# Row order of a gated FFN's hidden values, sums for the norms gathered by other instructions, and x quantised between a weight's steps

## The chip, the cores and the metric

The kernel runs on one core of a Trainium2 chip. The metric is the device time of one launch in microseconds (us). The core has a matmul engine (TensorE, PE in the profile), a vector engine (VectorE, DVE), a scalar engine (ScalarE, ACT), GpSimd (POOL) and SyncE (SP), which here only issues transfers. Each engine works through its own list of instructions in order; they wait for each other on semaphores.

## The reference, cut to what matters

Thirty-two sequences of 512 tokens with 256 channels go through two fake-quantised feed-forward blocks with a state-space layer between them.

```python
def fp4_quant_dequant(x):           # blocks of 16 along the last dimension
    xb = x.reshape(shape[:-1] + (shape[-1] // 16, 16))
    scale = max(max(abs(xb)) / 6.0, 1e-12)
    q = GRID[searchsorted(MID, abs(xb / scale))] * sign(xb) * scale
def fp4_linear(x, w): return fp4_quant_dequant(x) @ fp4_quant_dequant(w).T
def ffn(x): return fp4_linear(silu(fp4_linear(x, w_gate)) * fp4_linear(x, w_up), w_down)   # 256 -> 704 -> 256
def ssm(x):                          # 16 states a channel, a scan over 512 tokens
    Bm, Cm = split(x @ W_in + b_in); dt = softplus((x @ W_dt1 + b_dt1) @ W_dt2 + b_dt2)
    h[t] = exp(A * dt) * h[t-1] + expm1(A * dt) / A * Bm * x;  return sum(h * Cm) + D * x
x = x + 0.5 * ffn(layernorm(x)); x = x + ssm(layernorm(x)); x = x + 0.5 * ffn(layernorm(x))
```

A layernorm here subtracts the mean of a token's 256 channels and divides by sqrt(variance + 1e-5).

## The kernel before, in words

**Start.** SP loads the constants, the three weights and the first x. DVE quantises `w_gate`, `w_up` and `w_down` one after the other (L645 to L722), PE transposes each, ACT and DVE split the result into a high and a low f16 part. GpSimd finds the largest scale over all partitions by `partition_all_reduce` (L464, L468, L470, L475) and takes one power (L472). Only then does `body(-1, ...)` run on each engine: the first x is normalised and quantised, SP transposes it (`turn_x`), and PE begins its first product (L1200).

**Iterations.** After that there are 34 iterations. An iteration holds five stages of different sequences: A, the first FFN of sequence `it`; R, the norm and the small projections of the same sequence; S, the scan of sequence `it - 1`; C, the second FFN of sequence `it - 2`; N, load, norm and quantisation of the x of sequence `it + 1`. The first iterations lack S and C, the last ones lack A, R and N. The order of the work is written out by hand in `ORDER`, one list of pieces an engine: `A.am2`, say, is piece 2 of `am` (the maxima of the hidden values) in stage A. Every engine walks its list once an iteration.

**A norm.** DVE takes `bn_stats` of four groups of 128 tokens (L768), aggregates them (L774), and makes variance plus epsilon (L776) and the negated mean (L777), all in `stats`. GpSimd raises the variance to -1/2 and multiplies (`norm`, L481, L483). ACT writes the normalised x (`normalise`, L1017). There are three norms for a sequence: f (N and C, buffers `f_...`) and s (R, buffers `s_...`).

**Quantisation of the hidden values.** DVE multiplies gate and up into `hid` (`hidden`, L823), which lies by position: element `i` of all 44 blocks, then element `i + 1` of all. This comes from the order in which the rows of `w_gate` and `w_up` are loaded (L378). `amax_h` (L828) takes a maximum over each block, `scales_h` scale and reciprocal, GpSimd multiplies by the reciprocals (`values_h`, L529) and rounds by adding and taking off a magic number (`round_h`, L537, L545), and the grid value times the scale's high part (DVE, `high_h`, L846) and low part (GpSimd, `low_h`, L560) gives `qh`. SP transposes `qh` (`turn_h`) for the product with `w_down` (L1214). DVE adds the residual (`ffn_residual`, L857).

**The rest of R and S.** PE transposes the norm's output into `gu_ps` (L1224), projects (L1230), and ACT takes the result (`take_rBC`, L1057). DVE splits C into a high part (L882) and a low part (L885) in `split_C`, and `times_B` multiplies C and B (L875). Softplus and `make_dt` give dt. For each of 16 states and 2 halves, PE makes differences (L1274), ACT a decay (L1104), DVE the scan (L912) and the product with C (L922), PE adds it up in `y_ps` (L1294). At the end `take_y` adds `x_s` (L931). The bank pair `gu_ps` is shared by all gate and up products, the transposes of R and its projections; a new A begins when `dt` is made.

Of the kernel before, what the change touches and what calls it, by code (L numbers as in the profile page):

```python
# [28 lines left out]
    S.k0 S.c0 S.k1 A.gu0 S.w0 S.w1 A.gu1 S.w2 A.gu2 S.e0 S.w3 A.gu3 S.w4 S.w5 S.c1 S.e1 S.p0 S.w6 A.gu4 A.gu5  # L29
    S.p1 A.gu6 S.c2 S.p2 S.p3 S.w7 S.w8 S.p4 S.p5 S.c3 A.gu7 S.w9 C.gu0 S.w10 S.c4 S.p6 S.p7 C.gu1 S.p8 A.dn0  # L30
    S.w11 S.w12 A.dn1 S.c5 C.gu2 C.gu3 S.w13 S.c6 S.p9 C.gu4 A.dn2 S.w14 S.w15 A.dn3 C.gu5 S.p10 S.c7 S.p11
    S.p12 S.p13 S.p14 S.w16 S.w17 S.c8 C.gu6 S.w18 C.gu7 S.w19 S.c9 R.xt0 S.w20 S.p15 S.p16 S.p17 S.w21 S.w22
# [4 lines left out]
    S.k0 S.k1 C.ln0 A.hid0 S.g0 S.g1 A.hid1 C.xa0 C.xa1 C.xs0 S.p0 A.hid2 S.g2 S.g3 S.p1 C.xm0 S.g4 C.xm1 A.am0
    A.hid3 A.am1 S.p2 A.qs0 A.hid4 S.g5 S.p3 A.hid5 S.g6 C.qy0 C.qy1 A.qm0 S.p4 S.p5 A.qm1 S.g7 A.hid6 S.g8
    A.qv0 A.hid7 A.am2 S.p6 S.p7 C.hid0 A.am3 A.qs1 A.qv1 S.p8 S.g9 S.g10 A.qm2 S.p9 A.res0 A.qm3 S.g11 C.hid1
    S.g12 A.qv2 C.am0 A.res1 C.hid2 S.p10 S.p11 C.hid3 C.am1 A.qv3 C.qs0 S.g13 C.hid4 S.p12 S.p13 A.res2 S.g14  # L40
# [1317 lines left out]
```

## Time and profile before

| | |
|---|---|
| median of 3 runs | 3940.95 us (3935.68 to 3943.92) |
| the profiled execution | 3939.07 us, its span 3937.3 us |
| DVE busy | 3663.4 us, 93% |
| PE busy | 3345.5 us, 85% |
| GpSimd busy | 2834.5 us, 72% |
| ACT busy | 2735.2 us, 69% |
| mean granted TensorE clock | 0.956 of full speed |

Busy time is the union of an engine's instructions. A matmul's end is modelled, so that PE's busy time is not time at its peak. The whole span holds a start of some 120 us, in which little overlaps, then the iterations.

### The profile page before, as it was taken

What the parts mean: (1) busy time and instruction counts of PE and PEld (TensorE: products, weight loads), DVE (VectorE), ACT (ScalarE), POOL (GpSimd) and SP (SyncE); (2) the same over time, 40 slices, a digit from 0 to 9 for tenths busy, and PEclk for the clock granted to TensorE, in tenths of its full rate; (3) what the DMA queues carried; (4) which work ended last, traced back from release to release, by engine and by line L of the source; (5) the groups of instructions that cost most, each with busy time, mean ns of one, the idle gap of its engine ahead of it and who ended that gap; (6) DMA issues with size and microseconds to landing.
All of it is one profiled execution on the core that took longest, in us unless ns stands there. A gap on an engine that the chain in (4) does not pass through costs nothing. (4 is left out here: it accounts for less than half of the span.)

```text
span 3937.3 us, 79115 instructions
## 1 busy us (share of the span) xinstructions
PE 3345.5 (85%) x28716; PEld 2377.4 (60%) x28716; DVE 3663.4 (93%) x6091; ACT 2735.2 (69%) x5258; POOL 2834.5 (72%) x2296
## 2 busy tenths in 40 slices
PE   0478988988998888889889888988889988888985
PEld 0256666666666666666666666666666666666663
DVE  6489999999999999999999999999999999999995
ACT  0267777777677777777777777777777777777772
POOL 1447777787777778777777877777877777787755
PEclk9789999999999999999999999999999999999997
DMA  1111222222222222222222122222222222322212
GB/s 30 28 32 43 56 47 49 57 44 52 52 55 52 47 60 41 55 52 55 49 49 60 40 56 52 47 52 55 44 52 56 51 52 47 60 42 54 47 37 45
DMA packets 583041, 192.04 MB, mean 49 GB/s; under 512 B 544061, under 2 KB 578302, under 8 KB 582654
## 3 DMA queue, kind: packets, MB, share of 16 engines
q1 hardware_dynamic: 582654, 186.98, 23.3%
q8 instruction: 230, 3.77, 0.4%
q14 instruction: 157, 1.29, 0.1%
HBM read 19.16 MB, written 16.78 MB: 9 GB/s over the span
## 5 line engine op out<-in xcount | busy, mean ns | idle before, releaser
L1200 PE MATMUL gu_ps<-wgu,qxT 128*128 128x352 f16 x6144 | 1093.0, 329 | 197.5 <-DVE hid L823 94.8
L912 DVE TENSOR_TENSOR_SCAN state<-w_ps,decay 128x512 f32<-128x512 f32 x1024 | 1212.3, 1207 | 35.1 <-ACT decay L1104 22.8
L1200 PEld LDWEIGHTS gu_ps<-wgu,qxT 128*128 128x128 f16 x6144 | 587.2, 102 | 621.9 <-DVE hid L823 162.2
L1274 PE MATMUL w_ps<-bdif,x_parts 128*128 128x129 f16 (+1 forms) x12288 | 858.6, 224 | 78.6 <-DVE state L912 70.6
L1274 PEld LDWEIGHTS w_ps<-bdif,x_parts 128*128 128x128 f16 x12288 | 775.0, 100 | 170.7 <-issue 134.5
L1104 ACT ACTIVATE decay<-dt,A_sb 128x512 f32<-128x512 f32 x1024 | 677.8, 712 | 128.7 <-DVE state L912 101.1
L922 DVE SCALAR_TENSOR_TENSOR c_state<-state,inv_A,rep_ps 128x512 f32<-128x512 f32 x1024 | 726.2, 735 | 1.6 <-PE rep_ps L1284 0.4
L498 POOL TENSOR_TENSOR bdif<-dif,B_lo 128x516 f16<-128x516 f16 x512 | 531.6, 1055 | 188.9 <-PE w_ps L1274 188.9
L1092 ACT ACTIVATE bdif<-dif,B_tok 128x129 f16<-128x129 f16 x2048 | 629.1, 394 | 0.9 <-PE w_ps L1274 0.9
L1294 PE MATMUL y_ps<-ident,c_state 128*128 128x128 f32 x4352 | 605.4, 279 | 27.9 <-DVE c_state L922 27.9
L1214 PE MATMUL dn_ps<-wd,qhT 128*128 128x256 f16 (+1 forms) x4608 | 587.1, 277 | 36.6 <-DMA qhT<-qh 33.8
L1044 ACT ACTIVATE gate<-gu_ps,w_back 128x352 f32<-128x352 f32 x512 | 282.0, 551 | 413.2 <-PE gu_ps L1200 409.1
L1294 PEld LDWEIGHTS y_ps<-ident,c_state 128*128 128x128 f32 x4352 | 472.3, 141 | 151.7 <-DVE c_state L922 75.4
L1214 PEld LDWEIGHTS dn_ps<-wd,qhT 128*128 128x128 f16 (+1 forms) x4608 | 420.4, 99 | 167.7 <-issue 71.6
L537 POOL TENSOR_TENSOR val<-val,magic 128x704 f32<-128x704 f32 x256 | 396.3, 1548 | 129.0 <-DVE magic L853 129.0
L529 POOL TENSOR_TENSOR val<-hid,recip 128x704 f32<-128x704 f32 x256 | 430.6, 1703 | 15.3 <-DVE recip L839 15.1
L545 POOL TENSOR_TENSOR grid<-val,magic 128x704 f16<-128x704 f32 x256 | 402.9, 1574 | 20.1
L560 POOL TENSOR_TENSOR qh<-grid,scale_lo 128x704 f16<-128x704 f16 x256 | 372.0, 1463 | 4.7
L828 DVE TENSOR_REDUCE amax<-hid 128x44 f32<-128x704 f32 x256 | 370.1, 1446 | 2.3
L823 DVE SCALAR_TENSOR_TENSOR hid<-gu_ps,up_back,gate 128x352 f32<-128x352 f32 x512 | 291.2, 569 | 37.2 <-PE gu_ps L1200 26.6
L1284 PE MATMUL rep_ps<-C_parts,pick_row 48*128 48x512 f16 x512 | 199.9, 390 | 110.3 <-DVE c_state L922 110.0
L481 POOL TENSOR_TENSOR f_rstd<-f_var,minus_half 128x4 f32<-128x4 f32 x64 | 65.1, 1017 | 275.9 <-DVE f_neg L777 268.6
(153 smaller groups left out, 3695.5 us busy)
## 6 DMA issues: line engine op xcount, KB each, us to landing
x_in<-in_L_attn_x SPq DMA_DIRECT2D x32, 512.0 KB, 3.8
x_s<-x_a SPq DMA_DIRECT2D x32, 512.0 KB, 3.5
out<-x_out SPq DMA_DIRECT2D x32, 512.0 KB, 4.0
qhT<-qh SPq DMA_TRANSPOSE x256, 3.7
qxT<-qx SPq DMA_TRANSPOSE x128, 3.1
hid<-in_L_ffn_w_gate SPq DMA_DIRECT2D x2, 352.0 KB
bdif<-in_L_ffn_w_up SPq DMA_DIRECT2D x2, 352.0 KB
val<-in_L_ffn_w_down SPq DMA_DIRECT2D x1, 704.0 KB, 11.2
```

What stands on the lines that cost most here:

```text
L498: g.tensor_tensor(bdif[:, n % NB, :, 1, 0:P + 1], dif[:, 0:P + 1].unsqueeze(1).broadcast_to([P, T, P + 1]), B_lo[:, seq % 2, :, n:n + 1].b ...
L529: g.tensor_tensor(val[:, t % 2].rearrange("p (i b) -> p i b", b=HB), hid[:, t, :].rearrange("p (i b) -> p i b", b=HB), recip[:, t * HB:(t ...
L537: g.tensor_tensor(val[:, s], val[:, s], magic[:, s], ALU.add).then_inc(grid_h.sem, 1)
L545: g.tensor_tensor(grid[:, s], val[:, s], magic[:, s], ALU.subtract).then_inc(grid_h.sem, 1)
L912: v.tensor_tensor_scan(state[:, n % 2, gi, :], w_ps[:, gi, :], decay[:, n % 2, gi, :], 0.0, ALU.add, ALU.mult).then_inc(state_ready.sem, 1)
L922: v.scalar_tensor_tensor(c_state[:, n % 2, gi, :], state[:, n % 2, gi, :], inv_A[:, gi, n:n + 1], rep_ps[:], ALU.mult, ALU.mult).then_inc( ...
L1092: last = a.activation(bdif[:, n % NB, t, 0, 0:P + 1], dif[:, 0:P + 1], ACT.Copy, scale=B_tok[:, seq % 2, t, n:n + 1])
L1104: a.activation(decay[:, n % 2, gi, :], dt[:, seq % 2, gi, :], ACT.Exp, scale=A_sb[:, gi, n:n + 1]).then_inc(decay_ready.sem, 1)
L1200: last = te.matmul(gu_ps[:, m, 0:FH], qxT[:, t // 2, 4 * (t % 2) + xp * G + c], wgu[:, c, wp, a:a + FH], start=begin, stop=end)
L1214: last = te.matmul(dn_ps[:], qhT[0:k, t % 2, hp * FC + c, :], wd[0:k, c, wp, :], start=begin, stop=end)
L1274: last = te.matmul(w_ps[:, gi, t * P:t * P + wide], x_parts[:, seq % 2, xp, t, gi * P:(gi + 1) * P], bdif[:, n % NB, t, bp, 0:wide], start ...
L1294: last = te.matmul(y_ps[:, t // 2, col:col + P], c_state[:, n % 2, gi, t * P:(t + 1) * P], ident[:], is_transpose=True, start=(j, t % 2) = ...
```

## The change

- `hid`, `val`, `grid` and `qh` lie in natural order, the 16 elements of a block next to each other. `w_gate` and `w_up` are loaded in plain row order, by one transfer each where there were two. `amax_h` reads runs of 16; in `values_h`, `low_h` and `high_h` the scale or reciprocal of a block is an operand whose innermost step is 0 (before, the middle dimension had the step 0).
- `stats` is gone. The sum of a token's channels comes from an accumulator output: of `ffn_residual` for A (`a_sum`), of `take_y` for C (`c_sum`), which is four instructions of 256 columns instead of two of 512, and of four new ACT instructions for N (`sm`, `n_sum`). GpSimd makes the negated mean (`mean`, piece `mn`). ACT squares x minus mean with an accumulator output (`sq`, four instructions a norm). GpSimd makes variance plus epsilon, the power and the product (`norm`).
- C's high part is written by ACT (`high_C`, piece `ch`); DVE writes the low part only (`low_C`) and waits for ACT.
- In the start, x's norm stands before the quantisation of the weights on ACT and GpSimd; DVE takes the maxima and scales of x before the maxima of `w_down`, the magic of x after that of `w_down`, and the last product (`qy`) before `w_down`'s exponent; GpSimd's `xv` and `mx` stand between its reductions.
- `ORDER` is a new list for every engine.

```diff
     "DVE": """
-    S.k0 S.k1 C.ln0 A.hid0 S.g0 S.g1 A.hid1 C.xa0 C.xa1 C.xs0 S.p0 A.hid2 S.g2 S.g3 S.p1 C.xm0 S.g4 C.xm1 A.am0
...
-    S.g15 A.res3 R.ln0 C.qm0 S.p14 N.ln0 C.qm1 C.hid5 S.p15 C.am2 S.g16 S.g17 S.p16 C.hid6 S.p17 S.g18 C.qv0
+    S.k0 S.k1 S.g0 S.g1 S.p0 A.hid0 S.p1 C.xa0 C.xa1 A.hid1 C.xs0 A.am0 S.g2 A.hid2 S.g3 S.p2 S.g4 S.p3 C.xm0
...
+    C.qm0 C.hid4 A.res2 C.qm1 C.hid5 S.p14 S.p15 C.am2 C.qv0 A.res3 C.hid6 S.p16 S.p17 S.g18 C.hid7 C.qv1 C.am3
     "ACT": """
+    S.b0 S.b1 S.b2 S.d0 S.d1 C.sq0 S.d2 A.gu0 C.ln0 A.gu1 A.gu2 S.d3 S.b3 S.d4 S.d5 S.d6 C.ax0 C.ax1 S.d7 S.d8
...
+    S.b10 S.b11 S.b12 C.gu6 R.sq0 C.gu7 S.d20 S.d21 S.d22 N.sm0 S.d23 C.ah2 R.ln0 N.sq0 S.d24 S.d25 C.sh1 R.xt0
+    N.ln0 S.b13 R.rb0 S.d26 C.ah3 S.d27 R.ch0 S.b14 S.b15 S.d28 S.d29 S.d30 N.ax0 N.ax1 S.d31 R.z0 R.xh0
     "POOL": """
+    A.mh1 A.qp0 A.sl1 A.mv2 A.mv3 A.qp1 A.mh2 A.mh3 A.qp2 S.bl8 S.bl9 A.qp3 C.sl0 C.mv0 C.mv1 C.mh0 C.mh1 R.mn0
+    S.bl10 C.qp0 C.qp1 R.ln0 S.bl11 C.mv2 N.mn0 S.bl12 S.bl13 C.mh2 N.ln0 C.sl1 S.bl14 S.bl15 C.mv3 C.qp2 C.mh3
...
-                for i in range(2):
-                    sp.dma_start(w_raw[m][i * HB:(i + 1) * HB, 0:NR * DM].rearrange("p (r k) -> p r k", k=DM),
-                                 w.rearrange("(b r i) k -> i b r k", r=NR, i=2)[i]).then_inc(w_in[m].sem, 16)
+                sp.dma_start(w_raw[m][0:WR, 0:NR * DM].rearrange("p (r k) -> p r k", k=DM),
+                             w.rearrange("(r p) k -> p r k", p=WR)).then_inc(w_in[m].sem, 16)
...
-            def norm(unit, var, neg, rstd, nmr, ln, done, xhat):
-                pool.wait_ge(ln.sem, ln.at(unit, 10))
+            def mean(unit, sums, neg, done, xhat):
                 if not first(unit):
                     pool.wait_ge(xhat.sem, xhat.at(unit - 1, T))
+                g.tensor_tensor(neg[:], sums[:], minus_share[:], ALU.mult).then_inc(done.sem, 1)
+            def norm(unit, sq, var, neg, rstd, nmr, squared, done, up=1.0):
+                pool.wait_ge(squared.sem, squared.at(unit, T))
+                g.tensor_scalar(var[:], sq[:], up ** -2.0 / DM, LN_EPS * up ** -2.0, ALU.mult, ALU.add).then_inc(done.sem, 1)
+                pool.wait_ge(done.sem, done.at(unit, 2))
                 g.tensor_tensor(rstd[:], var[:], minus_half[:], ALU.pow).then_inc(done.sem, 1)
...
-                v.tensor_reduce(amax[:, t * HB:(t + 1) * HB], hid[:, t, :].rearrange("p (i b) -> p b i", b=HB), AX.X, ALU.max,
+                v.tensor_reduce(amax[:, t * HB:(t + 1) * HB], by_block(hid[:, t, :], HB), AX.X, ALU.max,
                                 apply_absolute_value=True).then_inc(qh_step.sem, 1)
...
-                v.tensor_tensor(qh[:, t, 0, 0:F].rearrange("p (i b) -> p i b", b=HB),
-                                grid[:, t % 2].rearrange("p (i b) -> p i b", b=HB),
-                                scale_hi[:, t * HB:(t + 1) * HB].unsqueeze(1).broadcast_to([P, BLOCK, HB]),
-                                ALU.mult).then_inc(qh_hi.sem, 1)
+                v.tensor_tensor(by_block(qh[:, t, 0, 0:F], HB), by_block(grid[:, t % 2], HB),
+                                per_block(scale_hi[:, t * HB:(t + 1) * HB]), ALU.mult).then_inc(qh_hi.sem, 1)
...
-                v.scalar_tensor_tensor(dst[:, t, :], dn_ps[:], down_back[:, 0:1], src[:, t, :],
-                                       ALU.mult, ALU.add).then_inc(ffn_done.sem, 1)
+                v.scalar_tensor_tensor(dst[:, t, :], dn_ps[:], down_back[:, 0:1], src[:, t, :], ALU.mult, ALU.add,
+                                       accum_out=None if sums is None else sums[:, t:t + 1]).then_inc(ffn_done.sem, 1)
...
-                v.tensor_scalar(C_parts[0:N, seq % 2, :], gu_ps[ROW_C:PR, 0, :], b_C[0:N, :], None,
-                                ALU.add).then_inc(C_step.sem, 1)
-                dve.wait_ge(C_step.sem, C_step.at(seq, 1))
+                dve.wait_ge(C_hi.sem, C_hi.at(seq, 1))
...
-                for b in range(G):
-                    v.tensor_tensor(x_c[:, 2 * b:2 * b + 2, :], x_s[:, 2 * b:2 * b + 2, :],
-                                    y_ps[:, b, :].rearrange("p (t d) -> p t d", d=DM), ALU.add).then_inc(y_done.sem, 1)
+                for t in range(T):
+                    v.scalar_tensor_tensor(x_c[:, t, :], y_ps[:, t // 2, t % 2 * DM:(t % 2 + 1) * DM], 1.0, x_s[:, t, :],
+                                           ALU.mult, ALU.add, accum_out=c_sum[:, t:t + 1]).then_inc(y_done.sem, 1)
...
+            def sums(it):
+                act.wait_ge(x_loaded.sem, x_loaded.at(it, 16))
+                for t in range(T):
+                    a.activation(f_xh[:, t, :], x_in[:, t, :], ACT.Identity,
+                                 accum_out=n_sum[:, t:t + 1]).then_inc(n_summed.sem, 1)
+            def squares(unit, src, neg, xh, sq, norm, squared):
+                act.wait_ge(norm.sem, norm.at(unit, 1))
+                for t in range(T):
+                    a.activation(xh[:, t, :], src[:, t, :], ACT.Square, bias=neg[:, t:t + 1],
+                                 accum_out=sq[:, t:t + 1]).then_inc(squared.sem, 1)
...
+            x_first = order("POOL", "N")
+            body(-1, [p for p in x_first if p[1] in ("mn", "ln")], None, None, 0)
+            for m in range(2):
+                pool.wait_ge(w_step.sem, W_STEPS * m + 4)
+                g.partition_all_reduce(w_top[:, m:m + 1], w_max[:, m:m + 1], P, bass.bass_isa.ReduceOp.max).then_inc(w_all.sem, 1)
+            body(-1, [p for p in x_first if p[1] == "xv"], None, None, 0)
+            pool.wait_ge(w_step.sem, W_STEPS * 2 + 4)
+            g.partition_all_reduce(w_top[:, 2:3], w_max[:, 2:3], P, bass.bass_isa.ReduceOp.max).then_inc(w_all.sem, 1)
+            body(-1, [p for p in x_first if p[1] == "mx"], None, None, 0)
+            pool.wait_ge(h_step.sem, 6)
+            g.partition_all_reduce(h_top[:], w_norm[:], P, bass.bass_isa.ReduceOp.max).then_inc(w_all.sem, 1)
+            pool.wait_ge(h_step.sem, 7)
+            g.tensor_tensor(h_bound[:], h_bound[:], h_half[:], ALU.pow).then_inc(w_all.sem, 1)
+            pool.wait_ge(bc_step.sem, 3)
+            g.partition_all_reduce(bc_top[:], bc_bound[:], P, bass.bass_isa.ReduceOp.max).then_inc(w_all.sem, 1)
```

## Rows read from the trace of the kernel before

**Rows 1.** Busy time by engine in one stretch: stretch, length, busy and count each
```profile
1504.20:1619.74 115.54, 103.09 (x898) 73.47 (x897) 111.94 (x189) 85.30 (x164) 88.06 (x72) 0.97 0.24 51
```

**Rows 2.** Timeline of DVE: start, us, engine, line and operation
```profile
1504.20 1.44 DVE L828 TENSOR_REDUCE amax<-hid 128x44 f32<-128x704 f32 x1
...
1619.74 1.44 DVE L828 TENSOR_REDUCE amax<-hid 128x44 f32<-128x704 f32 x1
```

**Rows 3.** DVE busy over the span of L768, L774, L776, L777, in this order
```profile
0.00:3938.00 3938.00, 134.73 (x384) 0.96 0.24 49
0.00:3938.00 3938.00, 36.64 (x384) 0.96 0.24 49
0.00:3938.00 3938.00, 38.80 (x96) 0.96 0.24 49
0.00:3938.00 3938.00, 15.39 (x96) 0.96 0.24 49
```

**Rows 4.** Groups of DVE instructions: form, count, busy us, mean ns, idle before
```profile
L828 DVE TENSOR_REDUCE amax<-hid 128x44 f32<-128x704 f32 x256 | 370.1, 1446 | 2.3
L846 DVE TENSOR_TENSOR qh<-grid,scale_hi 128x704 f16<-128x704 f16 x256 | 136.3, 532 | 5.8 <-POOL grid L545 5.8
L784 DVE TENSOR_REDUCE x_amax<-f_xh 128x32 f32<-128x512 f32 x128 | 85.6, 675 | 20.8 <-ACT f_xh L1017 19.0
L857 DVE SCALAR_TENSOR_TENSOR x_out<-dn_ps,down_back,x_c 128x256 f32<-128x256 f32 x128 | 60.6, 473 | 9.7 <-PE dn_ps L1214 9.7
L768 DVE BATCH_NORM_STATS2 f_stats<-x_in 128x6 f32<-128x256 f32 x128 | 45.0, 414 | 23.5 <-DMA x_in<-in_L_attn_x 23.5
L931 DVE TENSOR_TENSOR x_c<-x_s,y_ps 128x512 f32<-128x512 f32 x64 | 40.9, 680 | 0.6 <-PE y_ps L1294 0.6
L882 DVE TENSOR_SCALAR C_parts<-gu_ps,b_C 16x512 f16<-16x512 f32 x32 | 24.0, 751 | 1.0
...
L664 DVE TENSOR_TENSOR state<-val,recip 128x704 f32<-128x704 f32 x2 | 1.7, 889 | 0.0
...
L650 DVE TENSOR_REDUCE amax<-val 128x88 f32<-128x1408 f32 x1 | 1.6, 1608 | 0.0
```

**Rows 5.** Groups of ACT and GpSimd instructions, the same columns
```profile
L1017 ACT ACTIVATE f_xh<-x_c,f_nmr,f_rstd 128x256 f32<-128x256 f32 x128 | 66.2, 589 | 24.5 <-POOL f_nmr L483 24.5
L1026 ACT CAST scale_hi<-scale 128x88 bf16<-128x88 f32 x128 | 33.8, 264 | 311.6 <-DVE scale L836 311.6
...
L529 POOL TENSOR_TENSOR val<-hid,recip 128x704 f32<-128x704 f32 x256 | 430.6, 1703 | 15.3 <-DVE recip L839 15.1
...
L537 POOL TENSOR_TENSOR val<-val,magic 128x704 f32<-128x704 f32 x256 | 396.3, 1548 | 129.0 <-DVE magic L853 129.0
```

**Rows 6.** Timeline of DVE, then of PE, along the chain through `gu_ps`
```profile
1528.37 0.48 DVE L857 SCALAR_TENSOR_TENSOR x_a<-dn_ps,down_back,x_in 128x256 f32<-128x256 f32 x1 [0.32 <-PE dn_ps L1214]
...
1544.64 1.06 PE L1224 MATMUL gu_ps<-ident,s_xh 128*128 128x128 f32 x8
...
1584.31 3.11 PE L1200 MATMUL gu_ps<-wgu,qxT 128*128 128x352 f16 x12 [1.08 <-DMA qxT<-qx]
...
1589.13 1.95 PE L1200 MATMUL gu_ps<-wgu,qxT 128*128 128x352 f16 x12
1590.92 0.84 PE L1274 MATMUL w_ps<-bdif,x_parts 128*128 128x129 f16 x12
```

**Rows 7.** Timeline of GpSimd in the start
```profile
75.58 0.95 POOL L470 PARTITION_ALL_REDUCE h_top<-w_norm  x1
90.75 0.60 POOL L472 TENSOR_TENSOR h_bound<-h_bound,h_half 128x1 f32<-128x1 f32 x1 [14.22 <-DVE h_bound L726]
97.21 0.38 POOL L475 PARTITION_ALL_REDUCE bc_top<-bc_bound  x1 [5.86 <-issue]
104.84 1.05 POOL L481 TENSOR_TENSOR f_rstd<-f_var,minus_half 128x4 f32<-128x4 f32 x1 [7.25 <-issue]
```

**Rows 8.** Timeline of PE: the first gate and up products
```profile
121.69 12.84 PE L1200 MATMUL gu_ps<-wgu,qxT 128*128 128x352 f16 x66 [32.11 <-DMA qxT<-qx]
```

More of the change, by code:

```diff
@@ new lines, in hidden @@
+            def hidden(q, k):
+                t, cols = k // 2, slice(k % 2 * FH, (k % 2 + 1) * FH)
+                if not first(q) and k % 2 == 0:
+                    dve.wait_ge(val_ready.sem, val_ready.at(q - 1, t + 1))
+                dve.wait_ge(gu_ready.sem, gu_ready.at(q, 2 * k + 2))
+                dve.wait_ge(silu_ready.sem, silu_ready.at(q, k + 1))
+                v.scalar_tensor_tensor(hid[:, t, cols], gu_ps[:, 1, 0:FH], up_back[:, 0:1], gate[:, cols], ALU.mult,
+                                       ALU.mult).then_inc(hid_ready.sem, 1)
@@ new lines, in make_dt @@
+            def make_dt(seq):
+                dve.wait_ge(soft_step.sem, soft_step.at(seq, 4 * G))
+                if before(seq, 2):
+                    dve.wait_ge(decay_ready.sem, decay_ready.at(seq - 2, G * N))
+                for gi in range(G):
+                    v.scalar_tensor_tensor(dt[:, seq % 2, gi, :], soft[:, gi, :], 1e-7, gu_ps[:, gi, :], ALU.max,
+                                           ALU.add).then_inc(dt_ready.sem, 1)
+                dve.wait_ge(dt_ready.sem, dt_ready.at(seq, G))
+                v.tensor_scalar(dt[:, seq % 2], dt[:, seq % 2], 1e6, None, ALU.min).then_inc(dt_ready.sem, 1)
@@ L639, in _ @@
+            x_first = order("DVE", "N")
             w_val = state[:].rearrange("p a g l -> p (a g l)")
@@ L992, in _ @@
-            body(-1, order("DVE", "N"), None, None, 0)
             body(0, order("DVE", "ARN"), 0, None, 1)
@@ L1057, in take_rBC, with high_C @@
                 a.activation(rBC[:], gu_ps[0:PR, 0, :], ACT.Identity, bias=b_rBC[0:PR, :]).then_inc(r_ready.sem, 1)
+            def high_C(seq):
+                act.wait_ge(rB_ps.sem, rB_ps.at(seq, 1))
+                if before(seq, 2):
+                    act.wait_ge(rep_full.sem, rep_full.at(seq - 2, N))
+                a.activation(C_parts[0:N, seq % 2, :], gu_ps[ROW_C:PR, 0, :], ACT.Identity,
+                             bias=b_C[0:N, :]).then_inc(C_hi.sem, 1)
             def softplus(seq):
@@ L1111, in body @@
                 for stage, step, k in pieces:
-                    if step == "ln" and stage == "R":
+                    if step == "sm":
+                        if not first(pass_n):
+                            act.wait_ge(qx_ready.sem, qx_ready.at(pass_n - 1, 4))
+                        sums(it + 1)
+                    elif step == "sq" and stage == "R":
                         if not first(it):
@@ L1140, in body @@
                         high_scales(q[stage], k)
-            body(-1, order("ACT", "N"), None, None, 0)
+            x_first = order("ACT", "N")
+            body(-1, [p for p in x_first if p[1] != "ax"], None, None, 0)
+            for u, (m, c, cuts, dst, k) in enumerate(units):
+                if m == 2 and c == 0:
+                    body(-1, [p for p in x_first if p[1] == "ax"], None, None, 0)
+                act.wait_ge(w_tr.sem, w_tr.at(0, u + 1))
+                act.wait_ge(w_step.sem, W_STEPS * (m + 1))
+                for i, (c0, w) in enumerate(cuts):
+                    a.activation(dst[i][:, 0], gu_flat[0:k, c0:c0 + w], ACT.Copy,
+                                 scale=w_up_by[0:k, m:m + 1]).then_inc(w_hi.sem, 1)
             body(0, order("ACT", "ARN"), 0, None, 1)
```

504 lines of the change are left out of this document (237 added, 267 removed).

## The prediction

> **What bounds the kernel now.** I read the page's busy shares first (DVE 93%, all others under 86%), then the busy times of a stretch in the middle, then DVE's groups, then the timelines. The same instruction of the scan-and-FFN pattern returns after 1619.74 - 1504.20 = 115.54 us [rows 2]: that is one iteration, the period. In it DVE is busy 111.94 us, PE 103.09, GpSimd 88.06, ACT 85.30 [rows 1]. DVE idles 3.60 us a period; nobody else is that full. So in the middle the time is DVE's work, and a microsecond taken off DVE is a microsecond, as long as another engine can follow. The start, until PE's first product at 121.69 us [rows 8], is a chain of its own.
>
> **The change on DVE, a sequence at a time** (totals of the run divided by 32 sequences):
>
> - The statistics go: 134.73 + 36.64 + 38.80 + 15.39 = 225.56 us [rows 3], 7.05 a sequence. The wait for x_in ahead of them, 23.5 us or 0.73, leaves DVE too [rows 4]; ACT waits for x_in in its place, with slack.
> - C's high part goes: 24.0 us and 1.0 idle, 0.78 a sequence. ACT writes it first now and DVE's two readers wait for it. Behind them on DVE stand scans and products of S (S.p24, S.g26), on PE the projection z. ACT's instruction stands after a wait on rep_full that is an iteration old; I cost the wait at nothing.
> - The maximum over a block: now 1446 ns for 704 columns read at a stride of 44. Reads in natural order cost 675 ns for 512 columns and 1608 for 1408 [rows 4]. The line through both gives 1.04 ns a column and 675 + 192 x 1.04 = 875 ns for 704. Ends: 1608 / 2 = 804 and 675 x 704 / 512 = 928. I take 875: 8 x 0.571 = 4.57 us less.
> - The product with the scale's high part: 532 ns in f16 now. With an innermost step of 0 on the scale no 16-bit row exists; the nearest by pattern and length is the same product of w_down's quantisation in f32, 889 ns [rows 4]. Ends: 532 (nothing changes) and 889. I take the upper one, the row with that pattern: 8 x 0.357 = 2.86 us more.
> - take_y becomes four instructions of 256 columns out of PSUM. The residual C, the same form, is busy 60.6 / 128 = 0.473 us each; 4 x 0.473 - 40.9 / 32 = 0.61 more.
> - Eight accumulator outputs a sequence (residual A, take_y). No row shows one. Ends: 0, and 15.39 / 96 = 0.16 us for a short instruction of four columns [rows 3]. I take 0.10: 0.80 more, ends 0 and 1.28.
>
> Sum: -7.05 - 0.73 - 0.78 - 4.57 + 2.86 + 0.61 + 0.80 = -8.86 us. DVE then needs 111.94 + 3.60 - 8.86 = 106.7 us with today's idle time.
>
> The Trainium skill has a rule on the fourth item that speaks against the change. Vector Engine (DVE) Microarchitecture Reference, section 5.1 "Performance modes — why throughput varies by op and dtype": with 2-byte operands, two sources run two elements a cycle, but one element read 16 times as a source was seen to run at one. No run here shows it. By the rule the item is the 2.86 us above; if it didn't hold, the period would be 2.86 us shorter.
>
> **The other engines.** ACT gains 12 squares and 4 sums of 128x256. The same shape costs it 66.2 / 128 = 0.517 us [rows 5]: 16 x 0.517 = 8.3. Its 16 accumulator outputs: 0 to 0.264 us each, the whole of a short cast; I take 0.15, 2.4 us. C's high part: no more than 0.75, what DVE paid. ACT goes from 85.3 to 96.7 (94 to 98.6). GpSimd gains three means and three variances; its power of four columns costs 1.05 us [rows 7], the upper end for each; for a product I take 0.3, 1.8 us in all. And its product by the reciprocal can fall from 1703 ns to the 1548 of a plain add or stay [rows 5], worth 0 to -1.2 us; a stride that it dislikes could cost up to as much again. I take 89. PE has no less to do. Its 103.09 us hold slack: twelve gate and up matmuls take 3.11 us after a wait and 1590.92 - 1589.13 = 1.79 in a dense stretch [rows 6], so fewer waits give some back.
>
> All four are then between 89 and 104 us of 106.7. Lists that are walked in order can't keep DVE at 97% with the others so close: a late matmul or silu is now seen by DVE. I allow 1.5 us of new idle time (ends 0 and 5, the latter half of PE's and ACT's lost slack). Period 108.2, 7.3 us less.
>
> **How many periods.** From 121.69 to 3937.3 us there are 33.0 periods. In the first and the last iteration DVE waits anyway. A and R are saved in iterations 0 to 31, C in 2 to 33: I count 30.5. 30.5 x 7.3 = 223 us.
>
> **The start.** x's quantisation, from about 100 to 121.69 us, goes in among the weights. That looks like 20 us. GpSimd is against it: it stood 5.86 us without work between a power and a reduction over partitions, and 7.25 us between that reduction and the next power, both with no one to wait for [rows 7]. The pause runs from the end of the instruction before (the power at 90.75 came without one, 14.22 us after its reduction). The new order on GpSimd is norm, two reductions, xv, reduction, mx, reduction, power, reduction. If every turn costs such a pause, these follow on each other: xv ends near 80, reduction at 86, mx begins at 93 and takes four instructions of 1.2 us, to 98; reduction near 104, power near 112, reduction near 118, DVE's constants, PE's first product at 120 to 121. Gain 1 us. If xv and mx turn freely, it is 14. I take 2, near the first, since xv and mx are tensor_tensor instructions as the power is, and it was the turn between such a one and the reduction that cost the pause both ways. A loss of 3 (the first reduction behind x's norm, with `w_gate` waiting for it) is the other end.
>
> **Sum.** 3939.07 - 223 - 2 = 3714 us. That starts from the profiled execution, 1.9 us under the median of the runs.
>
> **Rivals.**
>
> 1. ACT or PE becomes the bound. For it: ACT at 96.7 with its silu gates waiting for PE, and PE's 103.09. Against: ACT idles 30 us a period now. ACT's own 96.7 plus half of its present 30.2 us of waits is 111.8; 3.7 x 30.5 = 113 less, 3824 with the start. PE bound, its busy time not shrinking and half of its 12.45 us of waits left, gives 109.3 and 3747, which is inside my own range.
> 2. The scale's product stays at 532 ns, and no new idle time comes: period 108.2 - 2.86 - 1.5 = 103.8; 30.5 x 11.7 = 357, 3580. PE's 103.09 stands against the whole of it; with PE at about 105.5 it is 3631.
> 3. The maximum doesn't get faster (the reduction pays for something else than the stride): 4.57 more, period 112.8, 3853. The two natural rows agree too well for that.
> 4. Slower: the chain through gu_ps. From the last residual of A (1528.37) to R's transpose 16.3 us, from there to the next A's product (1584.31) 39.7, from that to the residual (1584.31 - 115.54 = 1468.77) 59.6: it closes in 115.6, the period, with unknown slack inside [rows 6]. The norm in it gets two more handovers (mean to GpSimd, squares to ACT), each behind a GpSimd or ACT instruction of about 1.5 us, the squares 2.1 and a variance: 5.5 us; A's maxima give 4 x 0.57 back and its products with the scale take 1.4. Net 4.6: if the slack is under 4.6 us the chain decides, and with none the period is 120.1 and the time 3939 + 139 = 4078. Slack from 0 to 4.6 covers 4078 down to no change. Against it: DVE's list holds other work at almost every wait, which says that the chain waits for DVE and not DVE for it.
>
> **Chances.** My forecast with its own range 3660 to 3770: 0.62. Rival 1 (ACT): 0.15. Rival 2: 0.11. Rival 3: 0.05. Rival 4: 0.07. The predicted time is 3714. The range is 3625 to 3805: it takes in the accumulators (0.80 and 0.48 us a period, 24 and 15 us), the maximum's ends, the idle ends and most of rival 2, part of rival 1. Faster by over 0.2% 0.93, within 0.2% 0.02, slower 0.05; 0.2% is about what a measurement of this kernel can tell.
>
> **What would show it.** In the changed kernel: L828's form near 875 ns; the scale's product near 889; DVE still over 94% busy in a period of about 108 us, near 104 us of work; ACT near 97; the number of DVE instructions a period falls by some 30 and grows by 10; GpSimd with gaps of 6 to 7 us between `mx`, reductions and power in the start, and PE's first product at about 120 us. Wrong would be: a period set by ACT (DVE's waits naming decay or gate), a DVE accumulator output of over 0.2 us, or PE's first product before 112 us.

## The result, and the profile after

The changed kernel takes 3746.57 us (median, 3735.34 to 3761.93) against 3942.43 us before: ratio 0.9508, 95% interval 0.9463 to 0.9553. The forecast was 3714 with 3625 to 3805, so the range held. The profiled execution took 3736.29 us, 22 us more than forecast. The page of the kernel after, its busy shares and granted clock:

```profile
PE 3284.5 (88%) x28716; PEld 2344.1 (63%) x28716; DVE 3393.4 (91%) x5419; ACT 2999.7 (80%) x6314; POOL 2878.0 (77%) x2489
...
PEclk9889999999999999999999999999999999999997
```

A period is the time from one write of `dt` by DVE to the next, one turn through the lists. Single periods of the kernel after vary from 106.5 to 111.8 us, so I compare 26 of them. Windows of the kernel before, then of the kernel after, between two writes of `dt` 26 periods apart: stretch, length, busy us (count) of PE, PEld, DVE, ACT and GpSimd, then the clock (full is 1), the DMA share and GB/s.

```profile
538.90:3549.24 3010.34, 2682.78 (x23297) 1913.87 (x23296) 2905.57 (x4864) 2218.80 (x4264) 2289.75 (x1846) 0.97 0.25 51
```
```profile
522.46:3354.71 2832.25, 2638.80 (x23298) 1890.94 (x23297) 2685.91 (x4318) 2431.59 (x5117) 2318.85 (x2001) 0.98 0.26 54
```

Divided by 26: the period went from 115.78 to 108.93 us. DVE's work went from 111.75 to 103.30, its idle time from 4.03 to 5.63. ACT went from 85.3 to 93.5, GpSimd from 88.1 to 89.2, PE from 103.2 to 101.5. With the prediction's count of 30.5 periods, 6.85 x 30.5 = 209 us come from the period; PE's first product is 5.7 us later (below); 3939.07 - 209 + 5.7 = 3735.8, and 3736.29 was profiled.

The groups that answer to [rows 4, 5], kernel after (form, count, busy us, mean ns, idle before):

```profile
L724 DVE TENSOR_TENSOR qh<-grid,scale_hi 128x704 f16<-128x704 f16 x256 | 240.7, 940 | 3.2 <-POOL grid L538 3.1
L706 DVE TENSOR_REDUCE amax<-hid 128x44 f32<-128x704 f32 x256 | 221.7, 876 | 2.4
L690 DVE TENSOR_TENSOR qx<-x_grid,x_scale_hi 128x512 f16<-128x512 f16 x128 | 70.1, 548 | 12.1 <-POOL x_grid L513 11.9 <-issue 0.2
L1021 ACT ACTIVATE f_xh<-x_in,f_neg 128x256 f32<-128x256 f32 x128 | 63.0, 494 | 5.5 <-POOL f_neg L468 5.5
...
L806 DVE SCALAR_TENSOR_TENSOR x_c<-y_ps,x_s 128x256 f32<-128x256 f32 x128 | 46.4, 418 | 1.0 <-PE y_ps L1331 1.0
L1021 ACT ACTIVATION_READ_ACCUMULATOR f_xh<-x_in,f_neg 128x1 f32 x128 | 24.0, 187 | 0.0
L806 DVE DVE_READ_ACCUMULATOR x_c<-y_ps,x_s 128x1 f32 x128 | 10.4, 81 | 0.0
```

The reader sees the maximum at 876 ns (1446 before), the product with the high scales at 940 (532), and each accumulator output as a row of its own. What ends DVE's waits now, in the same stretch (us in total, times, longest):

```profile
DVE state L787 <- PE w_ps L1311: 45.3, 27, 4.0
DVE hid L701 <- PE gu_ps L1237: 38.7, 50, 1.6
DVE x_out L733 <- PE dn_ps L1251: 21.9, 27, 2.0
```

All three name PE. At the turn of each of the 26 periods the scan waits for `w_ps`: 0.5 us in 11 of them, 1.7 in 8 and 3.3 to 4.0 in 7 (the 27th wait lies inside a period). All of these 7 begin like this (timeline of the kernel after, cut):

```profile
1503.23 2.13 POOL L480 TENSOR_TENSOR x_parts<-s_xh,x_parts 128x1024 f16<-128x1024 f32 x1 [0.42 <-ACT x_parts L1098]
1503.87 1.77 DVE L690 TENSOR_TENSOR qx<-x_grid,x_scale_hi 128x512 f16<-128x512 f16 x1
...
1507.54 1.96 PE L1331 MATMUL y_ps<-ident,c_state 128*128 128x128 f32 x8 [1.73 <-DVE c_state L797]
...
1513.68 3.70 PE L1237 MATMUL gu_ps<-wgu,qxT 128*128 128x352 f16 x12
...
1518.44 2.34 DVE L787 TENSOR_TENSOR_SCAN state<-w_ps,decay 128x512 f32<-128x512 f32 x2 [3.97 <-PE w_ps L1311]
```

DVE's 16-bit product of x with its scale takes 1.77 us instead of 0.42 and ends 0.3 us after GpSimd's instruction beside it. PE idles 1.73 us; the granted clock, 1.00 from 1505 to 1507.5, is then 0.50 (the lower of its two levels, 1.2 GHz) until 1517.5. Its twelve matmuls take 3.70 us there; in the next period, at clock 1.00, they take 1.96. DVE waits 3.97 us for PE.

The start, GpSimd and PE of the kernel after ([rows 7, 8]):

```profile
33.60 5.42 POOL L468 TENSOR_TENSOR f_neg<-n_sum,minus_share 128x4 f32<-128x4 f32 x1 [22.20 <-ACT f_xh L1015]
...
48.62 0.38 POOL L595 PARTITION_ALL_REDUCE w_top<-w_max  x1 [5.81 <-issue]
...
80.38 3.02 POOL L501 TENSOR_TENSOR x_val<-f_xh,x_recip 128x512 f32<-128x512 f32 x2 [21.68 <-DVE x_scale_hi L672]
89.55 3.81 POOL L599 PARTITION_ALL_REDUCE w_top<-w_max  x1 [6.15 <-DVE state L905]
100.09 1.14 POOL L509 TENSOR_TENSOR x_val<-x_val,x_magic 128x512 f32<-128x512 f32 x1 [6.73 <-issue]
...
110.68 0.37 POOL L602 PARTITION_ALL_REDUCE h_top<-w_norm  x1 [5.81 <-issue]
118.01 0.59 POOL L604 TENSOR_TENSOR h_bound<-h_bound,h_half 128x1 f32<-128x1 f32 x1 [6.96 <-issue]
124.65 0.38 POOL L607 PARTITION_ALL_REDUCE bc_top<-bc_bound  x1 [6.05 <-issue]
127.36 3.11 PE L1237 MATMUL gu_ps<-wgu,qxT 128*128 128x352 f16 x10 [17.01 <-DVE inv_A L996]
```

Six turns between a reduction over partitions and elementwise work, in either direction, leave GpSimd idle for 5.8 to 7.0 us each. Only at the seventh (x_val, after 21.68 us of waiting for DVE) does none show. DVE waits behind four of the six: 7.60, 9.45, 7.19 and 5.65 us. The Trainium skill (GPSIMD Engine Reference, section 2.1 "Instruction dispatch") gives about 6 us of code loading, without an instruction in the profile, for the first call of a freshly loaded kernel. The size agrees. That these pauses are such loading is not shown; what the rows do show, and the page does not say, is a pause of that size at each of these turns.

The rows show a second thing. The negated mean of four columns takes 5.42 us at 33.60, and the reduction at 89.55 takes 3.81. With x last (the run `e1b_x_last` below), without DVE's work beside them, they take 0.19 and 0.35. Both run beside DVE's products and sums of the weights, which follow each other without a gap, and each ends within 0.3 us of the end of one of these (the first of the two at 37.22 ends at 39.07):

```profile
37.22 3.58 DVE L924 TENSOR_TENSOR hid<-c_state,scale 88x1024 f32<-88x1024 f16 x2
...
91.43 1.68 DVE L924 TENSOR_TENSOR val<-c_state,scale 128x704 f32<-128x704 f16 x2
```

So of the 7.60 us that DVE waits for w_gate's reduction, some 5.2 (5.42 - 0.19) come from this hold (one engine's instruction kept waiting by the other's), by an estimate from these rows, and 3.4 more stand in the reduction of w_down.

### The profile page after: what moved, and what is told of

It reads as the page before. It is cut to its first block and busy times, and to the rows that moved or that the text cites. A ratio compares the mean times of both kernels' runs of the same rounds, so it can differ in the third digit from the quotient of the medians.

```text
span 3734.1 us, 79636 instructions
## 1 busy us (share of the span) xinstructions
PE 3284.5 (88%) x28716; PEld 2344.1 (63%) x28716; DVE 3393.4 (91%) x5419; ACT 2999.7 (80%) x6314; POOL 2878.0 (77%) x2489
## 5 line engine op out<-in xcount | busy, mean ns | idle before, releaser
L1237 PE MATMUL gu_ps<-wgu,qxT 128*128 128x352 f16 x6144 | 1034.9, 320 | 117.3 <-ACT gate L1054 50.1
L1311 PE MATMUL w_ps<-bdif,x_parts 128*128 128x129 f16 (+1 forms) x12288 | 844.5, 221 | 96.7 <-DVE state L787 89.7
L1311 PEld LDWEIGHTS w_ps<-bdif,x_parts 128*128 128x128 f16 x12288 | 748.4, 98 | 219.3 <-issue 175.5
L1331 PE MATMUL y_ps<-ident,c_state 128*128 128x128 f32 x4352 | 620.2, 279 | 18.1 <-DVE c_state L797 18.0
L530 POOL TENSOR_TENSOR val<-val,magic 128x704 f32<-128x704 f32 x256 | 410.2, 1602 | 163.5 <-DVE magic L729 163.5
L538 POOL TENSOR_TENSOR grid<-val,magic 128x704 f16<-128x704 f32 x256 | 443.8, 1734 | 20.1
L522 POOL TENSOR_TENSOR val<-hid,recip 128x704 f32<-128x704 f32 x256 | 378.6, 1493 | 31.0 <-DVE recip L717 29.8
L553 POOL TENSOR_TENSOR qh<-grid,scale_lo 128x704 f16<-128x704 f16 x256 | 353.4, 1385 | 0.4
L724 DVE TENSOR_TENSOR qh<-grid,scale_hi 128x704 f16<-128x704 f16 x256 | 240.7, 940 | 3.2 <-POOL grid L538 3.1
L1045 ACT ACTIVATE magic<-val 128x704 bf16<-128x704 f32 x256 | 197.4, 782 | 39.9 <-POOL val L522 36.2
```

What stands on the lines that cost most here:

```text
L522: g.tensor_tensor(val[:, t % 2].rearrange("p (b i) -> p b i", i=BLOCK), hid[:, t, :].rearrange("p (b i) -> p b i", i=BLOCK), recip[:, t * ...
L530: g.tensor_tensor(val[:, s], val[:, s], magic[:, s], ALU.add).then_inc(grid_h.sem, 1)
L538: g.tensor_tensor(grid[:, s], val[:, s], magic[:, s], ALU.subtract).then_inc(grid_h.sem, 1)
L1237: last = te.matmul(gu_ps[:, m, 0:FH], qxT[:, t // 2, 4 * (t % 2) + xp * G + c], wgu[:, c, wp, a:a + FH], start=begin, stop=end)
L1311: last = te.matmul(w_ps[:, gi, t * P:t * P + wide], x_parts[:, seq % 2, xp, t, gi * P:(gi + 1) * P], bdif[:, n % NB, t, bp, 0:wide], start ...
L1331: last = te.matmul(y_ps[:, t // 2, col:col + P], c_state[:, n % 2, gi, t * P:(t + 1) * P], ident[:], is_transpose=True, start=(j, t % 2) = ...
```

## The experiments

### The kernel itself again

> The changed kernel as it is, beside the others of this group. Expected: 3747 us, ratio 0.951 to the kernel before (0.946 to 0.955); the period of its steady part between 108.5 and 109.5 us, TensorE's first gate/up product at 127 us as in its first profile. If the stall at the turn of the period (TensorE idle, its granted clock falling) sets the spread of its runs, they lie between 3735 and 3762.

Measured: 3749.16 us (3735.14 to 3774.46), ratio 0.952 (0.9495 to 0.9546). This is the base of what follows. The median and the period are as expected, but the runs reach 3774, 12 us above the 3762 named; that the stall at the turn sets the spread stays a reading of single traces. In this run's profile 26 periods average 109.38 us, with 103.87 of DVE's work, where the first profile had 108.93 and 103.30. The same kernel thus differs by half a microsecond a period between two executions, and the differences below are no finer than that.

### Operations and order, one without the other

```diff
 # e6: the changed kernel with the lists of the kernel before; new pieces beside the old places
-    S.b0 S.b1 S.b2 S.d0 S.d1 C.sq0 S.d2 A.gu0 C.ln0 A.gu1 A.gu2 S.d3 S.b3 ...
+    S.b0 S.b1 S.b2 S.d0 S.d1 C.sq0 S.d2 A.gu0 S.b3 A.gu1 C.ln0 S.b4 A.gu2 ...
 # (the first list of ACT, cut; DVE, PE and GpSimd likewise)
 # e9: the kernel before with the lists of the changed one; C.ln0, R.ln0, N.ln0 kept on DVE
```

> The changed kernel's operations in the order of the kernel before on every engine (the new pieces put close ahead of where the old ones stood). Theory 1, the gain comes from VectorE's shorter work (8.9 us per period) and the new order only gives back part of what the longer chains of the statistics cost: period 109 to 111, total 3750 to 3810 (ratio 0.951 to 0.967). Rival, the old order leaves the squares, the statistics' products and the normalisation waiting on one another across three engines: period 113 or more, total above 3870.

> The kernel before with the changed kernel's order of pieces on every engine and nothing else of the change (VectorE's statistics stay, each put close ahead of where the normalisation needs it). In the group before, the new operations in the old order ran at 1.005 of the kernel before. Theory 1, operations and order only gain together, VectorE being full here: its 111.9 us of work a period leave room for at most 3.6 us, so 0.97 to 1.01 (3825 to 3980 us). Rival, the order does most of it by itself by having the waits for the products of TensorE gone: 0.955 to 0.97.

Measured: old order with the new operations 3959.85 us, ratio 1.0054 (1.0042 to 1.0066); new order with the old operations 4147.54 us, 1.0545 (1.0516 to 1.0573). For the old order the rival held (above 3870); for the old operations both expectations failed, the time being far above them. So neither half gains anything alone as tried here, with one placing of the pieces that the other list lacks. Windows over 26 periods, old order, then new order with old operations:

```profile
541.40:3572.19 3030.79, 2709.90 (x23297) 1960.56 (x23297) 2713.14 (x4317) 2430.32 (x5122) 2291.31 (x2002) 0.95 0.25 51
```
```profile
543.05:3737.15 3194.10, 2791.08 (x23298) 1981.87 (x23297) 3049.17 (x4863) 2226.19 (x4264) 2309.00 (x1847) 0.93 0.23 48
```

In the old order DVE has only 104.35 us of work a period but idles 12.2. Its waits there:

```profile
DVE hid L701 <- ACT gate L1054: 108.0, 52, 4.2
DVE magic L729 <- ACT magic L1045: 64.0, 26, 2.5
DVE c_state L797 <- PE y_ps L1331: 50.5, 26, 2.0
```

So 4.2 and 2.5 us a period are now waits for ACT, which is 80% busy (2430.32 of 3030.79 us). I read this as ACT being late by its list and not full; no run moves ACT's pieces alone. In the new order with the old operations it is DVE's work that grows, from 111.75 to 117.28 us a period with the same instructions: the product with the high scales takes 0.78 us in the mean instead of 0.51, the two products of x in sum 2.7 us a period more. DVE idles 5.57 us a period there, mostly for PE.

### What the natural order of h is worth

```diff
 # e5: the kernel before; e10: the changed kernel, the same edit reversed. Cut: the loads of w_gate and w_up
 # and GpSimd's products with the reciprocal and the low scale change in the same way
-v.tensor_reduce(amax[...], hid[:, t, :].rearrange("p (i b) -> p b i", b=HB), AX.X, ALU.max, ...)
+v.tensor_reduce(amax[...], hid[:, t, :].rearrange("p (b i) -> p b i", i=BLOCK), AX.X, ALU.max, ...)
-v.tensor_tensor(qh "p (i b) -> p i b", grid, scale_hi.unsqueeze(1).broadcast_to([P, BLOCK, HB]), ALU.mult)
+v.tensor_tensor(qh "p (b i) -> p b i", grid, scale_hi.unsqueeze(2).broadcast_to([P, HB, BLOCK]), ALU.mult)
```

> The kernel before with h in its natural order and nothing else of the change: w_gate's and w_up's rows as they come, the maximum over contiguous blocks, the three products with one scale per block read 16 times in a row; the order of all engines stays. In that order the packed product never waits for GpSimd (0.51 us in the mean), so VectorE's sum should change by the maximum (4.6 us less a period) and the product (3.3 us more): 1.2 us less. Theory 1, that sum is what the layout brings where its packed product is not blocked: 3900 to 3940 (ratio 0.99 to 1.0), where the same edit is worth 0.025 in the new order. Rival, the layout is worth as much in either order, 2 to 3%: 3820 to 3860.

> The changed kernel with h kept by position within the block, as in the kernel before (its maximum strided, 1446 ns for 876; VectorE's product with the high scales packed, about 510 ns for 940; GpSimd's value product 1684 for 1384 to 1493), all else of the change in. Theory 1, VectorE's time counts in full: 4.6 us more and 3.4 less, 1.2 us per period, and the clock as it is: 3785 us (ratio 0.961). Rival, the slow product disturbs GpSimd (its roundings take 2.0 to 2.2 us under it, 1.52 otherwise) and the clock more than VectorE's sum shows, so the packed one gives back what the maximum costs: 3700 to 3750 (0.94 to 0.951).

Measured: on the kernel before 3884.94 us, ratio 0.9876 (0.9852 to 0.9900), period 114.34, 1.4 us less, with 2.1 us less work of DVE (109.6 a period) where theory 1 had 1.2. 3885 us lies between the two expectations, 15 us below theory 1's range and 25 above the rival's. All new operations together in the old order gave 1.0054, so there the others of them lose more than this layout gains. Taken back from the changed kernel: 3840.64 us, 0.977 (0.9743 to 0.9796), 92 us worse than the changed kernel, outside both expectations. Its windows, and one product in its timeline; then two products of the kernel after:

```profile
529.10:3446.94 2917.84, 2620.59 (x23298) 1877.23 (x23297) 2847.91 (x4317) 2431.07 (x5123) 2330.28 (x2003) 0.99 0.25 53
```
```profile
2057.94 1.52 POOL L539 TENSOR_TENSOR grid<-val,magic 128x704 f16<-128x704 f32 x1
2058.08 1.76 DVE L725 TENSOR_TENSOR qh<-grid,scale_hi 128x704 f16<-128x704 f16 x1
```
```profile
1576.70 0.88 DVE L724 TENSOR_TENSOR qh<-grid,scale_hi 128x704 f16<-128x704 f16 x1
1576.74 2.22 POOL L538 TENSOR_TENSOR grid<-val,magic 128x704 f16<-128x704 f32 x1
...
1793.50 1.52 POOL L538 TENSOR_TENSOR grid<-val,magic 128x704 f16<-128x704 f32 x1
1793.66 2.11 DVE L724 TENSOR_TENSOR qh<-grid,scale_hi 128x704 f16<-128x704 f16 x1
```

DVE has 109.54 us of work a period, 6.2 more than with the natural order; a sum of unhindered durations says 1.2. The packed product, 0.46 us at its fastest, takes 0.83 in the mean: in 61 of 256 cases it starts while GpSimd makes the grid value (L539) and ends 0.4 us after it. The form that reads a scale 16 times is held as well: started 0.16 us after the rounding, it takes 2.11 us and ends 0.75 us after it. But that happens in only 6 of 256 cases in the kernel after. In 90 the rounding starts during the product (0.04 us behind it in the first pair of lines); 87 of these products take 0.88 to 1.08 us, and the rounding is the one that takes long (2.05 to 2.26 us instead of 1.52). So whichever of the two starts second is held, and the order of starts makes the price: here the slow form loses 0.11 us to the packed one (0.94 against 0.83), not 0.41, and nearly all of the maximum's 4.5 us is gain. Short single-source instructions of DVE take longer too (the 128x88 scale 0.60 us, 0.32 with the natural order; 1.1 us a period).

The Trainium skill (GPSIMD Engine Reference, section 8 "Key points") names contention of GpSimd with DVE instructions in a 2-port mode or with two SBUF inputs. The traces agree, for the packed form and for the slow one, which both have two inputs in SBUF. They add the size: the rest of the other engine's instruction, and 0.4 or 0.75 us.

### The scales in pairs

```diff
-a.copy(scale_hi[:, s], scale[:, s])
+a.copy(scale_hi[:, s], scale[:, s].unsqueeze(2).broadcast_to([P, 2 * HB, 2]))
 # DVE
-per_block(scale_hi[:, t * HB:(t + 1) * HB])
+scale_hi[:, t * HB:(t + 1) * HB].unsqueeze(2).broadcast_to([P, HB, BLOCK // 2, 2])
```

> The changed kernel with each high scale written twice side by side by ScalarE, so that VectorE's product of grid and high scale reads them in pairs (innermost step 1, two elements) instead of one element 16 times (innermost step 0). Theory 1, VectorE's time counts in full and a pair is enough for the fast rate: the product falls from 940 ns to about 532, 8 of them per period, 3.3 us less per period, period 105.6 and total about 3645 (ratio 0.925). Rival A, a pair is not enough: the product stays at 940, ratio 0.951 as the changed kernel. Rival B, the product falls but another engine's chain holds the period: it falls by under 1 us, total 3715 to 3747.

Measured: 3685.18 us, ratio 0.9359 (0.9343 to 0.9375), 64 us below the changed kernel. That is between theory 1 (3645) and rival B (3715 to 3747). Windows of 26 periods, then the two groups:

```profile
518.10:3302.44 2784.34, 2588.85 (x23298) 1869.66 (x23297) 2645.65 (x4318) 2434.04 (x5123) 2252.34 (x2003) 1.00 0.27 55
```
```profile
L538 POOL TENSOR_TENSOR grid<-val,magic 128x704 f16<-128x704 f32 x256 | 395.5, 1545 | 20.1
L725 DVE TENSOR_TENSOR qh<-grid,scale_hi 128x704 f16<-128x704 f16 x256 | 216.1, 844 | 3.1 <-POOL grid L538 3.1
```

A pair is enough for the fast rate: the median is 548 ns (884 single), as theory 1 had it. But the mean is 844, because 62 of 256 products start during GpSimd's rounding and take 1.6 us in the median. DVE saves 1.5 us a period against the first profile of the changed kernel (2.1 against the second), not 3.3. Of that only 0.6 is this product; x's two products, never held in this window, give 0.7, and `magic` 0.4. GpSimd's rounding falls from 1734 ns (kernel after) to 1545, and the clock stays at 1.00 in every period, which are now 106.4 to 108.2 us. The clock and the 1.5 us were not tried apart.

### A lighter ACT

```diff
-a.activation(xh[:, t, :], src[:, t, :], ACT.Square, bias=neg[:, t:t + 1], ...)
+a.activation(xh[:, t, 0:16], src[:, t, 0:16], ACT.Square, bias=neg[:, t:t + 1], scale=4.0, ...)
```

> The changed kernel with ScalarE's 12 sums of squares per sequence taken over 16 of the 256 columns (the variance is left incomplete). ScalarE has about 2 us less per period. Theory 1, ScalarE has room (93.5 of 108.9 us busy) and is not on the path: 0.945 to 0.953, within 20 us of the changed kernel. Rival, the squares stand in the path of the normalisation at the turn of each period and in TensorE's stall there: 1.5 to 2 us per period less, 3685 to 3700 (0.936 to 0.940).

Measured: 3724.84 us, ratio 0.947 (0.9447 to 0.9493); ACT has 91.5 us a period instead of 93.5, the period is 108.43 instead of 108.93. The ratio is in theory 1's range; the time is 24 us below the changed kernel run again, 4 more than it allowed, and all four runs lie below all ten of the changed kernel. A period gives back a quarter of what ACT lost (half, against the second profile's 109.38): ACT is not the bound, but its work is not quite free either.

### The start

```diff
 # e1b: on GpSimd all reductions and the power, then x; the same on DVE and ACT
 # e1: on GpSimd
+reduce(bc); reduce(w_gate)
 norm of x
-reduce(w_gate); reduce(w_up); x_val; reduce(w_down); round x; reduce(norms); power; reduce(bc)
+x_val; round x; reduce(w_up); reduce(norms); power; reduce(w_down)
```

> The changed kernel with the whole quantisation of the first x behind the weights' again, as in the kernel before; the steady part is the changed kernel's. Theory 1, moving x between the steps of w_down lost time by the turns of GpSimd and not by itself: with x last TensorE's first gate/up product stands at 120 to 125 us (121.7 in the kernel before, 127.4 in the changed one). Rival, the move gained 2 us or more as forecast and the loss lies in the sums that replace the statistics: first product at 129 us or later.

> The changed kernel with GpSimd's start put in another order: the reductions of the B/C bound and of w_gate first, then the whole quantisation of x, then the reductions of w_up and of the norms, the power, and the reduction of w_down last; VectorE's part of x between the steps of w_up. Theory 1, the start is set by GpSimd's pauses of 6 to 7 us at each turn between a reduction and elementwise work (five of them waited for by VectorE, 36 us in sum: 7.60, 9.45, 7.19, 5.65 and 5.53 on ScalarE): with the turns behind VectorE's work TensorE's first gate/up product falls from 127.4 us to 97 to 102, total 25 to 30 us less (ratio 0.944). Rival, the pauses are not tied to the turn but to the first use after idling or to every reduction: they stay, first product above 115 us, total within 12 us of the changed kernel.

Measured: PE's first product, x last, then regrouped:

```profile
122.36 7.88 PE L1226 MATMUL gu_ps<-wgu,qxT 128*128 128x352 f16 x39 [34.61 <-DMA qxT<-qx]
```
```profile
109.26 9.01 PE L1237 MATMUL gu_ps<-wgu,qxT 128*128 128x352 f16 x41 [1.27 <-DVE wd L978]
```

With x last it comes at 122.4, where theory 1 had 120 to 125: the move costs 5.0 us (127.4 - 122.4), the sums at most 0.7 (122.4 - 121.7). Its total, one execution of 3744.1 us, says nothing at this size. Regrouped it comes at 109.3: 18.1 us earlier, 7 short of the expectation; 3735.39 us, ratio 0.9479 (0.9456 to 0.9501), 14 us below the changed kernel where 25 to 30 were expected. A total within 12 us, as the rival had it, is narrowly missed too; its first product above 115 us is refuted. What was left, GpSimd of the regrouped start:

```profile
61.37 7.34 POOL L509 TENSOR_TENSOR x_val<-x_val,x_magic 128x512 f32<-128x512 f32 x1 [6.42 <-DVE x_magic L703]
...
79.56 0.38 POOL L594 PARTITION_ALL_REDUCE w_top<-w_max  x1 [5.77 <-issue]
```

The rounding took 7.34 us instead of 1.15, with no turn before it, beside six instructions of DVE for w_up back to back (61.41 to 70.44 us); then the turn followed behind it. That is the hold that the changed kernel's start shows twice, and neither theory had it.

### Together, and two swaps

```diff
 # e8: pairs and regrouped start.  e11: e8 with, on DVE,
-C.hid1 S.g13 C.am0 A.res0 A.qv2 C.hid2 ... C.am2 C.qv0 A.res3
+C.hid1 S.g13 C.am0 A.qv2 A.res0 C.hid2 ... C.qv0 C.am2 A.res3
 # e12: e11 with x's work on GpSimd behind reduce(w_up), the power last
```

> The scale pairs and the regrouped start together. If their gains add up (pairs 64 us; of the start, 17.5 us in the row of the first dt): 3668 us, ratio 0.931. If the start's gain is lost in the steady part: 3685, 0.936. With the pairs in, no period has TensorE's clock under 0.98, and the fastest ones take 106.4 us.

> Pairs and regrouped start as in the group before (3669 us, 0.933), with two neighbours swapped in VectorE's order: A's product with the high scales of the third group ahead of the residual, C's of the first group ahead of a maximum. In the trace these two wait about 1 us each for GpSimd's rounding to end (1.59 and 1.77 us instead of 0.55), 2 per period. Theory 1, the swap lets them in before that rounding starts and VectorE's time is on the path: up to 1.8 us per period less, 3615 to 3650. Rival, VectorE has as much slack as its waits show (about 4.5 us a period) or the wait only moves to GpSimd: 3660 to 3680.

> As the run before it in this group, with GpSimd's start in a third order: reductions of B/C and w_gate, the norm of x, reduction of w_up, the quantisation of x, then the reductions of the norms and of w_down and the power last; VectorE's products of x at the head of w_down. In the first regrouping two waits for a reduction were left (5.23 and 6.68 us), one because GpSimd's first rounding of x took 7.34 us beside VectorE's additions for w_up. Theory 1, both go: first gate/up product at 96 to 99 us (109.3), 10 to 13 us less than the run before it. Rival, the turn to the power (about 7 us) now ends last: 103 to 108 us.

Measured: e8 3669.29 us, 0.9331 (0.9309 to 0.9354), the sum of both gains (64 and 14). e11 3618.45 us, 0.9188 (0.9175 to 0.9202): 51 us for two swaps of neighbours, as theory 1 had it. e12 3607.39 us, 0.9164 (0.9150 to 0.9177), 11 us less, first product at 100.1, just outside theory 1's 96 to 99; the fastest version. Windows of e11:

```profile
494.86:3241.90 2747.04, 2580.05 (x23298) 1873.13 (x23297) 2590.51 (x4318) 2433.58 (x5123) 2255.17 (x2003) 1.00 0.27 56
```

DVE's work falls from 101.69 (e8) to 99.64 us a period, the product's mean from 0.83 to 0.56 us, and the period from 107.23 to 105.66. GpSimd's rounding rises from 1.54 to 1.61 us in the mean: part of the wait has moved to it.

## Why the prediction was right, and where it wasn't

- **DVE's sum: right, by its parts and partly by luck.** -8.1 of work forecast, -8.45 measured. Maximum 876 ns (875). Product 940 (889): +3.26 for +2.86. The rule of the Trainium skill about one element read 16 times (Vector Engine (DVE) Microarchitecture Reference, section 5.1) agrees with the runs: 0.83 us at the fastest, against 0.46 for the packed form and 0.51 for a pair. `take_y` +0.17 (+0.61), accumulator reads 81 ns, 0.65 (0.80). Not in the sum: `magic` -0.7 and x's products +0.7, which cancel by luck; in the seven long cases x's product ends 0.3 us after GpSimd's instruction beside it. The statistics, the largest term (7.05), were never put back alone in the new order: what they are worth in time is argued from this sum, where the layout's share was tried (e10).
- **ACT 96.7 forecast, 93.5 measured.** Squares 0.494 and sums 0.400 us (0.517), reads 0.187 (0.15), but a read begins before its ACTIVATE has ended, so busy time grows less than the durations add up to. Rival 1 (ACT) is refuted by the lighter ACT, which left the period at 108.4. GpSimd 89.2 (89).
- **The rival of a full PE was nearer in number.** Its 109.3 us and 3747 lie closer to the measured 108.9 and 3746.57 than my forecast. The mechanism is another: e11 swaps only pieces of DVE, PE's busy time stays within 0.5 us a period, and the period falls to 105.66.
- **New idle time: 1.5 forecast, 2.3 measured.** 4.03 us before held 0.72 of the wait for x_in, which is gone; 5.63 - 3.31 = 2.3. It is PE that DVE waits for, as forecast.
- **The step that failed in size is the start:** gain 2, measured loss 5.7. The pauses came as the every-turn case had them. What failed is the timetable they start from: x_val ended at 83.4 and not near 80, late behind DVE's 7.60 us of wait for w_gate's reduction, which I had named only as the loss end; and the next reduction took 3.8 us and not 0.4, held beside DVE. These 3.4 and 3.4 us carry the first product from 120 or 121 to 127.4. The hold between DVE and GpSimd stood nowhere in my sum. The start's 7.7 us and the period's 6.85 instead of 7.3 (14 us) make up the 22 between 3714 and 3736.
- **The step that was missing is the order.** I priced the lists at 1.5 us of idle time. The runs say that the new operations in the old lists leave DVE 12.2 us of idle time and are not faster at all, and that DVE's durations themselves depend on the list, by 5.5 us with the old operations, and by 4 in the price of the natural order (2.1 us of work less in the old list, 6.2 in the new one). My sum came out because the new list fits the new operations; from the profile of before, with an unfitted list, rival 4's "no change" would have been the result, though by waits that name ACT and not by the chain through `gu_ps`. (That this chain "closes in 115.6, the period" showed nothing: its third part was computed by taking the period off.)
- "A microsecond off DVE is a microsecond" held only roughly: in e11 2.05 us of work less gave 1.57 of period, in e10 6.24 us more cost 3.29.

## To carry to other kernels

Price an instruction by its duration beside what the neighbour engine does at that place, not by its mean: of a DVE product with two inputs and a GpSimd instruction the second to start waits for the rest of the first, and swapping neighbours can be worth nearly as much as a faster form (51 us against 64 here). New operations and a new hand-written order are one change: here each alone was slower (1.005 and 1.055). In a start, gather GpSimd's reductions and its elementwise work into few turns and put the turns behind other engines' work (first product 127.4, then 109.3, then 100.1 us).

## What the hardware showed beyond expectation

- One element read 16 times: 0.83 us at the fastest for 704 columns of 16 bits; the same read in pairs 0.51. GpSimd's rounding (L538) takes 2.0 us or more in 90 of 256 cases with the single form in the kernel, each time begun during that product, and in none of 256 with pairs.
- The single form that starts during a GpSimd instruction (a rounding or a product of 704 columns) ends 0.75 us after it, the packed one 0.4 us after it.
- A GpSimd addition of 512 columns took 7.34 us instead of 1.15 beside DVE's back-to-back products and sums of two inputs, in each of three traces (e1, e8, e11); a product of four columns took 5.42 instead of 0.19.
- Twelve matmuls took 3.70 us after a stall of 1.73 us, at a granted clock of 0.50, and 1.96 us at 1.00.
